# Two batches a stage apart between the gated attention and the experts, in a four-layer sandwich on one Trainium2 core

## The reference

```python
x = x + _layernorm(_L1_attn_ref(_layernorm(x, axis=-1), ...), axis=-1)
x = x + _layernorm(_L1_ffn_ref(_layernorm(x, axis=-1), ...), axis=-1)
x = x + _layernorm(_L2_attn_ref(_layernorm(x, axis=-1), ...), axis=-1)
x = x + _layernorm(_L2_ffn_ref(_layernorm(x, axis=-1), ...), axis=-1)
```

## Time and profile before

| quantity | value |
|---|---|
| median of 3 runs | 1621.38 us (1619.67 to 1626.66) |
| profiled execution, its own time | 1616.14 us |
| its span | 1614.3 us |
| gated attention (about) | 412 to 929 us |
| end of attention to first expert product | 929 to 1108 us |
| experts and rest | 1108 us to the end |
| busy share of the span: TensorE, ScalarE, VectorE, GpSimd | 80%, 71%, 67%, 17% |

### The profile page before, as it was taken

The page is one execution under the profiler, slowest core; times in us unless marked ns, Lnnn a source line. Parts: engine busy times, 40 slices in busy tenths (PEclk is TensorE's granted clock), DMA queues, the critical chain, the costliest instruction groups (busy, mean ns, idle before and its releaser), DMA issues.

```text
span 1614.3 us, 22138 instructions
## 1 busy us (share of the span) xinstructions
PE 1285.2 (80%) x8028; PEld 656.5 (41%) x8028; DVE 1079.6 (67%) x2031; ACT 1141.7 (71%) x1619; POOL 271.6 (17%) x361
## 2 busy tenths in 40 slices
PE   5588888876677777777777777687999997888996
PEld 2233333344111111111111144566777775666775
DVE  6878877054455665556555665546978788766898
ACT  3167776755899989999999934345565655977885
POOL 4500003042000000000000023274010134703000
PEclk9589999997588788878887899897999998999998
DMA  5611120002410101101000030002333334010111
GB/s 175 160 22 22 23 42 3 2 1 79 117 21 0 20 2 19 20 0 21 20 1 0 1 152 1 1 1 45 111 97 92 98 99 164 14 33 27 47 46 53
DMA packets 40765, 74.65 MB, mean 46 GB/s; under 512 B 6096, under 2 KB 10448, under 8 KB 39888
## 3 DMA queue, kind: packets, MB, share of 16 engines
q1 hardware_dynamic: 39792, 71.67, 15.8%
q10 hardware_dynamic: 864, 1.57, 0.3%
HBM read 59.26 MB, written 13.96 MB: 45 GB/s over the span
## 4 chain that ended last, share of the span: by engine, by line
PE 38%; ACT 25%; DVE 20%; issue 12%; POOL 2%; DMA 1%; SPq 0%; DVEq 0%; POOLq 0%; ACTq 0%
ACT SHARED L1035 14%; PE PS L823 4%; PE PS L992 4%; PE PS L979 3%; DVE SHARED L1045 3%; DVE NM L732 3%; PE PS L645 2%; PE PS L712 2%; PE PS L1767 2%; PE PS L787 2%; PE PS L1769 2%; PE PS L1768 2%; DVE KS L1922 2%; PE PS L1215 2%; PE PS L1776 2%
## 5 line engine op out<-in xcount | busy, mean ns | idle before, releaser
L1035 ACT ACTIVATE SHARED<-PS 128x1536 f32<-128x1536 f32 (+1 forms) x352 | 466.1, 1434 | 31.2 <-PE PS L979 30.2
L979 PE MATMUL PS<-QS,KS 51*128 51x512 bf16 (+1 forms) x1024 | 242.1, 461 | 134.1 <-ACT SHARED L1035 128.7
L1045 DVE TENSOR_TENSOR SHARED<-SHARED 128x1536 f32<-128x1536 f32 (+1 forms) x176 | 286.6, 1702 | 86.4 <-ACT SHARED L1035 86.4
L803 ACT ACTIVATE SHARED<-PS 128x512 f32<-128x512 f32 (+3 forms) x384 | 164.4, 493 | 93.8 <-PE PS L791 84.6
L979 PEld LDWEIGHTS PS<-QS,KS 51*128 51x128 bf16 (+1 forms) x1024 | 41.2, 99 | 386.8 <-ACT SHARED L1035 358.7
L992 PE MATMUL PS<-SHARED,Vg 128*16 128x512 f32 x1024 | 157.9, 694 | 1.7 <-DVE SHARED L1045 1.6
L732 DVE TENSOR_REDUCE NM<-PS 128x2 f32<-128x1024 f32 (+3 forms) x128 | 128.9, 1021 | 28.6 <-PE PS L718 20.5
L1767 PE MATMUL PS<-ROUNDED 128*128 128x512 f32 x328 | 137.1, 418 | 5.2 <-ACT KS L1868 4.5
L1769 PE MATMUL PS<-ROUNDED 128*128 128x512 f32 x328 | 131.5, 401 | 0.0
L1768 PE MATMUL PS<-ROUNDED 128*128 128x512 f32 x328 | 131.2, 400 | 0.0
L1856 ACT ACTIVATE ROUNDED<-KS 128x512 fp32r<-128x512 f32 x100 | 63.1, 631 | 86.0 <-DVE KS L1922 86.0
(11 more groups left out here) (265 smaller groups left out, 2280.6 us busy)
## 6 DMA issues: line engine op xcount, KB each, us to landing
SHARED<-wx SPq DMA_DIRECT2D x64, 256.0 KB, 3.2
qx<-SHARED SPq DMA_DIRECT2D x24, 256.0 KB, 3.9
SHARED<-in_moe SPq DMA_DIRECT2D x3, 1600.0 KB, 11.9
kx<-SHARED SPq DMA_DIRECT2D x18, 256.0 KB, 4.0
SHARED<-wx SPq DMA_DIRECT2D x16, 224.0 KB, 3.0
SHARED<-qx SPq DMA_DIRECT2D x16, 192.0 KB, 4.6
SHARED<-kx SPq DMA_DIRECT2D x16, 192.0 KB, 5.3
QS<-qx SPq DMA_DIRECT2D x16, 192.0 KB, 4.6
```

The source lines that it names most:

```text
L803: act.activation(PB[t % 3][:, h, q0:CH], bank(RING0[n % 3], q0), ACT.Exp, scale=SCORE_SCALE)\
L979: ins = pe.matmul(bank((v % 2) * GRP + f - a), KS[g % 2][r, h // 2, kt * P:kt * P + P], QS[g % 2][r, h // 2, qh * CH:(qh + 1) * CH], start ...
L1035: act.activation(dst, PS[:, (v % 2) * GRP * CH:((v % 2) * GRP + b - a) * CH], ACT.Exp if second == qh else ACT.Sigmoid, scale=SCORE_SCALE)\
L1045: dve.tensor_tensor(ex_tile(j), ex_tile(j), GR[w % RING][:, 0:(b - a) * CH], ALU.mult)\
```

## The change

The work stays the same; its order and some places change.

- During rounds 18 to 24 of the attention TensorE turns the first batch's attention output (18), projects it (20 and 22) and turns the next stage's input (24), all in bank 7. VectorE copies the turned tiles, GpSimd applies the norm for these two chunks (`pool_apply` is now a set of chunks). The GLU weights are loaded and dequantized there too, into another part of the arena.
- After the attention each engine has one program written out, `pe_between`, `act_between`, `dve_between`, `pool_between`, in which a step of one batch alternates with one of the other. Two chunks of a batch are taken through a product stage together, and down products follow both ups.
- `pool_keep` is called per chunk and no longer once for all. `pe_turn_x` moves out of `pe_ffn_up`. The 15 splits stand as 4, 5, 2 and, behind the routing weights, 4 (before: 2, 6, 3, 1, 1 and 2).

The diff, cut to its core:

```diff
+        def pe_beside_gated(pe, n, j):
+            if (n, j) == (18, 2):
+                pe.wait_ge(A[1, "ot_free"], QH * HG)
+                pe_turn_out(pe, 1, 0, 7)
+            if (n, j) == (18, 7):
+                pe.wait_ge(A[1, "aTs"], 1)
+                pe_turn_out(pe, 1, 1, 7)
+            if (n, j) == (20, 3):
+                pe.wait_ge(A[1, "ot_free"], QH * HG + 1)
+                pe_out_y(pe, 1, 0, "o1", RW["bo1"], 7)
+            if (n, j) == (22, 3):
+                pe.wait_ge(A[1, "ot_free"], QH * HG + 2)
+                pe_out_y(pe, 1, 1, "o1", RW["bo1"], 7)
+            if (n, j) == (24, 2):
+                pe.wait_ge(A[1, "ot_free"], QH * HG + 3)
+                pe_turn_x(pe, edges[3], 0)
+            if (n, j) == (24, 7):
+                pe.wait_ge(h_ready, edges[3].n_x(0))
+                pe_turn_x(pe, edges[3], 1)
+        def dve_beside_gated(dve, own, hf):
+            if hf == 9:
+                for c in range(QH):
+                    dve.wait_ge(A[1, "aT"], c + 1)
+                    dve.tensor_copy(chunk(hT, c), bank(7)).then_inc(A[1, "aTs"], 1)
+            if hf in (10, 11):
+                dve_y(dve, own, edges[3], hf - 10)
+                dve_x(dve, own, edges[3], hf - 10)
+            if hf == 12:
+                for c in range(QH):
+                    dve.wait_ge(xt_ready, edges[3].n_x(c))
+                    dve.tensor_copy(chunk(hT, c), bank(7)).then_inc(h_ready, 1)
+            if hf == 13:
+                dve.wait_ge(late_in[0], 16 * N_LATE[0])
+                dve.tensor_scalar(LF, LI, 1.0 / 127.0, None, ALU.mult).then_inc(A[3, "w"], 1)
...
-        def dve_gated(dve):
...
+                dve_beside_gated(dve, own, hf + 1)
                 dve.wait_ge(A[1, "pv"], KT * (hf + 1))
...
+                if g in (5, 6):
+                    pool_y(own, edges[3], g - 5)
+                    pool_x(own, edges[3], g - 5)
...
+                if g == HG + 1:
+                    sp.dma_start(LI, l1int).then_inc(late_in[0], 16)
...
-        LI = arena(0, 1152).bitcast(I32)
-        LF = arena(1152, 1152)
+        LI = arena(24576, 1152).bitcast(I32)
+        LF = arena(27648, 1152)
...
+        def pe_between(pe):
+            e3, e4, e4b = edges[3], edges[4], edges["4b"]
+            pe.wait_ge(A[1, "ot_free"], QH * NG)
+            pe_turn_out(pe, 1, 2, 0)
+            pe_turn_out(pe, 1, 3, 1)
+            pe_out_y(pe, 1, 2, "o1", RW["bo1"], 6)
+            pe_out_y(pe, 1, 3, "o1", RW["bo1"], 7)
+            pe.wait_ge(A[3, "w"], 1)
+            pe_glu_up(pe, 0)
+            pe_glu_up(pe, 1)
+            pe_glu_down(pe, 0)
+            pe_glu_down(pe, 1)
+            pe_turn_x(pe, e3, 2)
+            pe_turn_x(pe, e3, 3)
+            pe_glu_up(pe, 2)
+            pe_glu_up(pe, 3)
+            pe_glu_down(pe, 2)
+            pe_turn_x(pe, e4, 0)
+            pe_glu_down(pe, 3)
+            pe_turn_x(pe, e4, 1)
+            pe_features(pe, 0)
+            pe_features(pe, 1)
+            pe_kv(pe, 0)
+            pe_linear_out(pe, 0)
+            pe_linear_out(pe, 1)
+            pe_turn_x(pe, e4, 2)
+            pe_turn_x(pe, e4, 3)
+            pe_features(pe, 2)
+            pe_linear_turn(pe, 0)
+            pe_features(pe, 3)
+            pe_linear_turn(pe, 1)
+            pe_kv(pe, 1)
+            pe_linear_project(pe, 0)
+            pe_linear_project(pe, 1)
+            pe_linear_out(pe, 2)
+            pe_linear_out(pe, 3)
+            pe_turn_x(pe, e4b, 0)
+            pe.wait_ge(A[4, "o"], 2 * NC)
+            pe_ffn_up(pe, 4, e4b, L2A, 0)
+            pe_linear_turn(pe, 2)
+            pe_turn_x(pe, e4b, 1)
+            pe_ffn_up(pe, 4, e4b, L2A, 1)
+            pe_linear_turn(pe, 3)
+            pe_linear_project(pe, 2)
+            pe_ffn_down(pe, 4, L2B, HID4, RW["fc2b2"], 0)
+            pe_linear_project(pe, 3)
+            pe_ffn_down(pe, 4, L2B, HID4, RW["fc2b2"], 1)
+            pe_turn_x(pe, e4b, 2)
+            pe_turn_x(pe, e4b, 3)
+            pe_ffn_up(pe, 4, e4b, L2A, 2)
+            pe_ffn_up(pe, 4, e4b, L2A, 3)
+            pe_ffn_down(pe, 4, L2B, HID4, RW["fc2b2"], 2)
+            pe_ffn_down(pe, 4, L2B, HID4, RW["fc2b2"], 3)
...
+        def act_between(act):
...
+            act_attention_end(act, 1, (2, 3))
+            act_glu(act, 0)
+            act_glu(act, 1)
+            act_apply(act, e3, 2)
+            act_apply(act, e3, 3)
+            act_turned(act, e3, 2)
+            act_turned(act, e3, 3)
+            act_glu(act, 2)
+            act_apply(act, e4, 0)
+            act_glu(act, 3)
+            act_apply(act, e4, 1)
+            act_turned(act, e4, 0)
+            act_turned(act, e4, 1)
...
+            act_apply(act, e4b, 0)
+            act_turned(act, e4b, 0)
+            act_apply(act, e4b, 1)
+            ffn(0)
+            act_linear_turned(act, 2)
+            act_turned(act, e4b, 1)
+            ffn(1)
+            act_linear_turned(act, 3)
+            act_apply(act, e4b, 2)
+            act_apply(act, e4b, 3)
+            act_turned(act, e4b, 2)
+            act_turned(act, e4b, 3)
+            ffn(2)
+            ffn(3)
...
-                 3: Edge(3, 2, y_ready),
+                 3: Edge(3, 2, y_ready, y_at=(7, 7, 6, 7), t_at=(7, 7, 0, 1), pool_apply=(0, 1)),
...
+        def dve_between(dve, own):
+            e3, e4, e4b, e5 = edges[3], edges[4], edges["4b"], edges[5]
+            dve_y(dve, own, e3, 2)
+            dve_y(dve, own, e3, 3)
+            dve_glu(dve, 0)
+            dve_x(dve, own, e3, 2)
+            dve_x(dve, own, e3, 3)
+            dve_glu(dve, 1)
+            dve.memset(VF[:, :, D:D + 1], 1.0)
+            dve_y(dve, own, e4, 0)
+            dve_y(dve, own, e4, 1)
+            dve_x(dve, own, e4, 0)
+            dve_glu(dve, 2)
+            dve_x(dve, own, e4, 1)
+            dve_glu(dve, 3)
+            late(dve, 1)
+            dve_y(dve, own, e4, 2)
+            dve_y(dve, own, e4, 3)
+            dve_linear(dve, own, 0)
+            dve_x(dve, own, e4, 2)
+            dve_linear(dve, own, 1)
+            dve_x(dve, own, e4, 3)
+            dve_keep(dve, own, e4, 0)
+            dve_kv_blocks(dve, 0)
+            dve_keep(dve, own, e4, 1)
+            dve_linear_norm(dve, own, 0)
+            dve_linear_norm(dve, own, 1)
+            dve_linear(dve, own, 2)
+            dve_linear(dve, own, 3)
+            dve_kv_blocks(dve, 1)
+            dve_x(dve, own, e4b, 0)
+            dve_x(dve, own, e4b, 1)
+            dve_linear_norm(dve, own, 2)
+            dve_linear_norm(dve, own, 3)
+            dve_keep(dve, own, e4, 2)
+            dve_keep(dve, own, e4, 3)
+            dve_clear5(dve, own)
+            dve_x(dve, own, e4b, 2)
+            dve_y(dve, own, e5, 0)
+            dve_x(dve, own, e4b, 3)
+            dve_y(dve, own, e5, 1)
+            dve_x(dve, own, e5, 0)
+            dve_x(dve, own, e5, 1)
+            dve_y(dve, own, e5, 2)
+            dve_y(dve, own, e5, 3)
+            dve_x(dve, own, e5, 2)
+            dve_x(dve, own, e5, 3)
+        def pool_between(pool, pw):
...
+            pool_keep(pw, 0)
+            pool_keep(pw, 1)
+            pool_y(pw, e4, 2)
+            pool_y(pw, e4, 3)
+            pool_x(pw, e4, 2)
+            pool_x(pw, e4, 3)
+            pool_keep(pw, 2)
+            pool_keep(pw, 3)
+            late(pool, 2)
+            splits(4)
+            pool_x(pw, e4b, 0)
+            pool_x(pw, e4b, 1)
+            splits(5)
+            pool_x(pw, e4b, 2)
+            pool_y(pw, e5, 0)
+            pool_x(pw, e4b, 3)
+            pool_y(pw, e5, 1)
+            pool_x(pw, e5, 0)
+            pool_x(pw, e5, 1)
+            splits(2)
+            pool_y(pw, e5, 2)
+            pool_y(pw, e5, 3)
+            pool_x(pw, e5, 2)
+            pool_x(pw, e5, 3)
+            pool_rest_of_h(pool, 5, 0)
+            pool.wait_ge(A[5, "cw"], 1)
+            splits(4)
...
```

More of the change, by code:

```diff
@@ L241, in n_scale @@
             def n_scale(self, c):
-                return self.count(c, lambda e: e.turn and not e.pool_apply)
+                return sum(edges[n].turn and k not in edges[n].pool_apply
+                           for n, k in ORDER[:ORDER.index((self.name, c)) + 1])
             def y_tile(self, t):
@@ L355, in pool_edge @@
                     pool_x(own, e, s - 1)
-            if e.keep:
-                pool_keep(own)
+            for c in range(NC if e.keep else 0):
+                pool_keep(own, c)
         def act_apply(act, e, c):
@@ L648, in pe_y, with act_attention_end @@
                 ins.then_inc(ready or y_ready, 1)
-        def act_attention_end(act, L):
-            for c in range(NC):
+        def act_attention_end(act, L, chunks):
+            for c in chunks:
                 act.wait_ge(A[L, "aT"], c + 1)
@@ new lines, in pe_features @@
+        def pe_features(pe, c):
+            pe.wait_ge(h_ready, edges[4].n_x(c))
+            if c == 0:
+                late(pe, 1)
+            for i in range(3):
+                j = 3 * c + i
```

(57 more changed lines are left out.)

267 lines of the change are left out of this document (67 added, 200 removed).

## The result

| quantity | before | after |
|---|---|---|
| median (runs) | 1620.53 us (4) | 1597.13 us (4) |
| range of the runs | 1615.41 to 1626.66 | 1593.90 to 1603.26 |
| ratio, 95% interval | | 0.9865 (0.9822 to 0.9907) |
| profiled execution, its own time | 1616.14 us | 1603.26 us |
| its span | 1614.3 us | 1601.5 us |

The change makes the kernel 22 us faster (15 to 29 by the interval). A second comparison gave 0.9879 (0.9853 to 0.9906), 19.6 us.

What follows compares the result with a forecast made beforehand. ScalarE fills the attention; afterwards TensorE waits 45 us at draining stage boundaries. Overlap -17.5 us plus attention cost 3 gives -14.5: 1606.9 us on the median, range 1599 to 1616.

Steps and rivals of the forecast that it cites:

- The head: From attention's end to the first GLU product: one chunk's projection remains, so that product starts 9.8 us earlier.
- the last edge: From the last FFN y (1073.6) to the first expert product (1090.3); the sum of chunk 0 leaves VectorE's queue.
- the two named stalls: GLU: VectorE does sums and statistics before releasing bank 3; FFN: 3 us gap before turning chunk 3.
- (a): Between attention and experts, VectorE's fixed interleaving gives the gain back, leaving the head start: -6.8 us, chance 0.16.
- (c): Between attention and experts, batches wait for each other through shared banks, no overlap: about -2 us, chance 0.06.
- (d): In the attention, TensorE stops at the turn of OS behind VectorE's extra work: slower, +6.1 us, chance 0.06.
- Attention: Six inserted TensorE steps make score tiles late for ScalarE: 3 us in sum, bounds 0 and about 9.
- The fit that I computed for VectorE: In attention rounds, projection, edge and copy end at 13.3 us against OS's turn at 14.0: just fits.
- The rule on the shared ports: VectorE with two SBUF inputs and GpSimd exclude each other; attention applies would cost 1.5 us over the room per round.
- The stretch: From the end of the attention to the first expert product: 17.5 us shorter.
- (b): Between attention and experts, TensorE's clock stays up: 11 us less busy, half on the path, -20 us, chance 0.12.
- Splits: Experts: four splits instead of two behind the routing weights cost 0, or 1.1 us if they lengthen a VectorE operation.

Runs made afterwards that it cites:

- e1: Changed kernel with its six attention steps kept, the rest going stage after stage as in the kernel before: 1609.89 us, ratio 0.9954 to before.
- e2: Changed kernel without the six steps in the attention, interleaved programs kept: 1608.54 us, ratio 0.9949 to before.
- e10: Changed kernel with the down product of GLU chunk 0 ahead of chunk 1's up products: 1600.07 us, ratio 0.9897 to before.
- e3: Kernel before with 70 idle TensorE products in its gaps between attention and experts: 1614.32 us, ratio 0.9993 to before.
- e6: Changed kernel with two of the four splits behind the routing weights moved ahead of the last edge: 1592.29 us, ratio 0.9857 to before.

## Why the prediction was right or wrong

**Direction and place: right, size: too small.** The gain lies between the attention and the experts, and it comes from overlapped edges, as forecast. The head came 10.0 us earlier (9.8), the last edge took 16.7 us (1073.6 to 1090.3, 16.7), the two named stalls have 3.27 and 2.33 us. The conditions of (a), (c) and (d) did not come about: the distance shrank by 23.4 us, not by 9.8, and the attention's cost is 0.8 us.

**Attention: term mis-sized, +3 forecast, +0.8 measured** (e1 has it too, e2 has none). I charged every insert on top of a value group as lateness of ScalarE beyond half a microsecond in hand. ScalarE's idle time ahead of its tiles is 30.2 us in all in the profile of after, and it is 30.2 us in that of before: the inserts moved its waits and added none. Of the 0.8 us, about 0.5 is ScalarE's busy time (486.03 against 485.58 us); what lengthened it is not shown. The fit that I computed for VectorE was near, from the profile of after, at the second projection:

```profile
781.69 1.05 PE L645 MATMUL PS<-W,SHARED 128*128 128x128 f32 x8
...
785.57 1.13 DVE L283 SCALAR_TENSOR_TENSOR X<-PS,RSY,X 128x128 f32<-128x128 f32 x4 [1.48 <-POOL RSY L328]
...
787.93 0.66 DVE L1088 COPY OS<-PS 128x512 f32<-128x512 f32 x1
...
789.38 0.66 PE L1001 MATMUL PS<-ident,OS 128*128 128x128 f32 x4
```

Projection to the end of the copy is 6.9 us (5.9 plus the projection's own time forecast), and TensorE turned OS without a wait. The copy took 0.66 us against 0.69. The rule on the shared ports that the forecast took from the Trainium skill (SBUF — State Buffer, Who interferes with whom), by which the sum would have been -11.5, was not put to the test here. GpSimd's applies ran while VectorE had no operation with two inputs in SBUF, for its multiplications began later:

```profile
789.85 1.74 POOL L339 TENSOR_SCALAR XN<-X,NMX,RSX 128x128 f32<-128x128 f32 x4
...
795.19 17.91 DVE L1082 TENSOR_TENSOR SHARED<-SHARED 128x1536 f32<-128x1536 f32 x11 [4.54 <-ACT SHARED L1072]
```

**The stretch: -17.5 forecast, -23.4 measured.** The missing 5.9 us by segment, forecast against after: GLU 43.0 against 40.9 (2.1), features to key-value product 34.9 against 34.1 (0.8), key-value product to FFN 12.8 against 11.5 (1.3), FFN 41.9 against 40.2 (1.7), head and last edge as forecast within 0.2.

The step that failed is the size of this term, and in it the way in which products and handovers were added up. The forecast added the lengths of records where TensorE starts the next one sooner. Down and turn, twice, ahead of the features is the plainest case, 7.2 us forecast (2.84 + 0.66, twice, and 0.2) and 6.2 measured, 2.67 + 0.44 from start to start:

```profile
983.86 2.84 PE L645 MATMUL PS<-SHARED 128*128 128x128 f32 x24
986.53 0.60 PE L398 MATMUL PS<-ident,XN 128*128 128x128 f32 x4
986.97 2.84 PE L645 MATMUL PS<-SHARED 128*128 128x128 f32 x24
```

In the GLU this is 1.0 us; the products of the first two chunks give 0.6 (14.9 against 15.5), their downs 0.3 (5.4 against 5.7), the eight turns at 969.38 with their copy 0.3 (1.3 against 1.6), and the second batch's products took 0.2 more. In the features 0.3 lies ahead of the first key-value product and 0.5 between it and the second batch's features. In the FFN the up product of chunk 1 gives 0.4 (3.7 against 4.1) and the sixteen products at the end 0.5 (7.7 against 8.2); the gap came as forecast. Before the FFN the turn and copy of 1.1 us that I put behind the norms are hidden: TensorE turned at 1034.00, before the last norm, and its product waited for VectorE alone.

Little of the 5.9 us can be put down to the clock, entry by entry. I priced GLU and turns by rows at the upper level, so that a part of rival (b) was in my sum without being named. Only the first FFN chunk was priced by the slow 5.68 us; it took 5.1 us (1035.69 to 1040.83), a wait of 1.33 us included that was not forecast, so 0.6 of the 5.9 us is there. Then I gave (b) a chance of 0.12 because of "new gaps". The gaps came, and the clock stayed: 1.00 in the GLU in spite of its 3.27 us, 1.00 in the FFN in spite of 2.33 us. Had it been lost in the GLU, as in e2, that segment would be 3.0 us longer; had it been lost in the features, as in e10, 2.8 us. So my prices at the upper level came true by a clock for which I had given no reason.

Which share of the whole 23.4 us the clock has cannot be read off one run, since e3 shows that a higher clock is worth 2.6 us under the old order. (b), 1601.4 us, lies nearer to the measured medians, 1597.13 and 1599.14, than my forecast, and its 11 us less busy is what the profile shows. But that half of it is on the path was a guess that no run tests, and on top of a sum that held part of it already; the nearness of its time is in part luck.

**Splits: 0 taken, about +2 measured.** The bound of 1.1 us was too low. I priced two more splits by the VectorE operation beside them. What they did is push GpSimd's next work, the remainders, 5.5 us back, onto two VectorE operations that TensorE waits for (3.49 us against 1.33 in e6), and TensorE did 63 products in 20 us in place of 71 in the kernel before. With it one condition of error in the forecast was met ("if the experts lengthen by over 1 us"). Of the other two, ScalarE's idle time did not grow, and in the FFN VectorE is what TensorE waits for only ahead of the first product (1.09 us).

**The absolute number.** The forecast hung on the median of three runs, 1621.38 us; the kernel before had 1620.53, 1618.89, 1615.84 and 1618.06 in the four comparisons. The forecast missed by 9.8 us. The three terms above are 6.1 of it (5.9 + 2.2 - 2.0), the reference value 0.9 (1621.38 less 1620.53), and the other 2.8 us are within the interval of this comparison.

## What to carry over

Where every stage boundary drains, let two independent batches run a stage apart on all engines, and test the parts together as well as alone: those of this change are worth 7.5 and 9.3 us alone and 23.4 together. When pricing such a change, add products from start to start and not by the lengths of their records, note for each duration at which clock level its row was taken, and price the stretch at both levels as two cases. Work on GpSimd that is "free" by its due time still moves what GpSimd does next: look at which VectorE operations that will then stand beside, and whether TensorE waits for them.

## What had not been expected of the hardware

The same wait has two prices. Behind 3.27 us for VectorE in the GLU, the next pair of products took 1.13 us in after and 2.07 us in e2, whose instructions there are the same. What differed is what the engine did before: in after it ran at a granted clock of 1.00 from the end of the attention on, in e2 it had come out of a wait of 4.89 us 13 us before this one began. And a step that ends earlier can make the next one later: in e10 the features began 1.3 us earlier, at a clock of 0.82 in place of 0.90, and ended 1.5 us later. Nor does the longest wait tell whether the clock falls: in those features of e10 TensorE never waited over 2.3 us, and its clock was 0.82, while 3.27 us in the GLU of after left it at 1.00.
